# A four-layer graph network on one core: masks made four blocks ahead, left-over weights made in the first sweep and carried through DRAM, row sums in another PSUM bank, two kept pairs loaded early

## What is computed

```python
# layer 0
Ax = adj @ h;  x = x + 1 - 0.1 * h - 0.01 * sum(h * Ax, axis=1)
# layer 1: two hops
g = h
for k in range(2):
    g = tanh(concatenate([adj @ g, g], axis=1) @ W[k])
x = x + g
# layer 2: weights from the rank of a neighbour within its row
mask = (adj != 0);  rank = cumsum(mask, axis=1);  deg = rank[:, -1:]
k = minimum(deg, 100);  pos = rank - (deg - k)
w = mask * where(pos > 0, 0.5 ** (k - pos), 0)
x = x + w @ (h @ weight) + bias
# layer 3
u = tanh(concatenate([h, t]) @ W1 + b1) @ W2 + b2
XB = h @ B.T
x = x + u + adj @ XB - sum(adj, axis=1) * XB
```

## Time and profile before

| | |
|---|---|
| median of three runs | 791.98 us |
| the profiled execution, its own time | 788.66 us |
| its span | 786.6 us |
| PE, DVE, ACT, POOL busy | 91%, 60%, 23%, 21% |
| DMA | 280.96 MB, 357 GB/s mean |
| chain that ended last | PE 51%, DMA 31%, DVE 8%, POOL 4% |

### The profile page before, as it was taken

One profiled execution on the slowest core, in us unless ns is written; L12 is line 12 of the kernel. 1 busy time (PEld: TensorE's weight loads), 2 busy tenths in 40 slices (PEclk: granted clock), 3 DMA queues, 4 the chain that ended last, 5 costly groups with the idle time before them and its releaser, 6 DMA issues.

```text
span 786.6 us, 10295 instructions
## 1 busy us (share of the span) xinstructions
PE 714.9 (91%) x3752; PEld 287.1 (36%) x3752; DVE 468.5 (60%) x789; ACT 182.8 (23%) x279; POOL 168.7 (21%) x172
## 2 busy tenths in 40 slices
PE   1999999999899999999999967888888889999997
PEld 0333333333334333344444432333333333433333
DVE  5677666767988878555566625878888831111111
ACT  2000000000001000001010015777777731111111
POOL 5011110012000000012112232343454414222231
PEclk9999999999999999999999987999999999999999
DMA  9799999999999999999999948888999979999994
GB/s 372 312 423 420 421 419 420 421 418 366 345 387 408 385 383 374 379 358 359 362 370 367 350 192 330 328 309 316 341 349 339 330 247 373 351 369 369 367 367 191
DMA packets 48659, 280.96 MB, mean 357 GB/s; under 512 B 5985, under 2 KB 15329, under 8 KB 15713
## 3 DMA queue, kind: packets, MB, share of 16 engines
q1 hardware_dynamic: 38754, 271.39, 88.6%
q10 hardware_dynamic: 9856, 8.92, 3.5%
HBM read 275.56 MB, written 4.73 MB: 356 GB/s over the span
## 4 chain that ended last, share of the span: by engine, by line
PE 51%; DMA 31%; DVE 8%; POOL 4%; issue 4%; ACT 1%; SPq 0%; ACTq 0%; DVEq 0%; POOLq 0%
PE accA L993 34%; DMA land<-adj_blocks 15%; DMA cache<-adj_blocks 8%; DMA uS<-counts 5%; PE spare L1025 4%; DMA xin<-x_rows 3%; PE accA L1036 3%; DVE uS L835 2%; PE nat L926 2%; PE tr L902 2%; POOL rstd L495 2%; PE spare L1008 1%; PE nat L922 1%; DVE uS L825 1%; PE nat L918 1%
## 5 line engine op out<-in xcount | busy, mean ns | idle before, releaser
L993 PE MATMUL accA<-land,X 128*64 128x512 f32 x1536 | 370.1, 600 | 10.7 <-DMA land<-adj_blocks 7.8
L825 DVE TENSOR_TENSOR uS<-uS,land 128x512 f32<-128x512 f32 x192 | 133.1, 693 | 65.4 <-DMA land<-adj_blocks 56.1
L993 PEld LDWEIGHTS accA<-land,X 128*64 128x64 f32 x1536 | 103.0, 137 | 187.6 <-issue 136.2
L835 DVE TENSOR_SCALAR uS<-land 128x1024 bf16<-128x1024 f32 (+1 forms) x192 | 134.2, 747 | 53.6 <-DMA land<-adj_blocks 52.6
L993 PE MATMUL accA<-cache,X 128*64 128x512 f32 x512 | 126.5, 602 | 15.2 <-DVE X L867 12.5
L502 POOL TENSOR_TENSOR hS<-tS 128x256 f32<-128x256 f32 x32 | 25.6, 802 | 475.5 <-DVE tS L706 475.5
L407 ACT ACTIVATE wS<-spare 128x1024 uint16<-128x1024 f32 x112 | 108.6, 1033 | 56.2 <-PE spare L1025 56.0
L1025 PE MATMUL spare<-uS,triA 128*128 128x512 bf16 x256 | 78.5, 389 | 30.7 <-DMA uS<-counts 11.0
L1036 PE MATMUL accA<-wS,X 128*128 128x512 bf16 x256 | 77.7, 386 | 0.0
L583 ACT ACTIVATE rowsT<-tr 128x256 f32<-128x256 f32 x40 | 15.4, 385 | 236.2 <-PE tr L902 236.2
L993 PEld LDWEIGHTS accA<-cache,X 128*64 128x64 f32 x512 | 36.6, 138 | 83.2 <-issue 76.9
(11 more groups left out here) (78 smaller groups left out, 465.8 us busy)
## 6 DMA issues: line engine op xcount, KB each, us to landing
land<-adj_blocks SPq DMA_DIRECT2D x240, 1024.0 KB, 7.6
cache<-adj_blocks SPq DMA_DIRECT2D x16, 1024.0 KB, 12.3
xin<-x_rows ACTq DMA_DIRECT2D x32, 128.0 KB, 5.5
x_rows<-zS ACTq DMA_DIRECT2D x24, 128.0 KB, 5.0
cache<-x_rows SPq DMA_DIRECT2D x1, 1024.0 KB, 4.9
loadjS<-adj_blocks SPq DMA_DIRECT2D x64, 8.0 KB
uS<-counts SPq DMA_DIRECT2D x64, 4.0 KB
out_rows<-zS ACTq DMA_DIRECT2D x8, 128.0 KB, 7.3
```

The costliest lines, as they stand in the source:

```text
L825: nc.vector.tensor_tensor(total, total, of[:, i * W:(i + 1) * W], ALU.add)\
L835: nc.vector.tensor_scalar(masks(b)[0:rows, :], block_of(p, c, b)[0:rows, :], 0.0, None, ALU.not_equal)\
L993: last = nc.tensor.matmul(accA[k * D:(k + 1) * D, c % 2, :], tile(X[p % 2], TQ * b + k), of[:, k * W:(k + 1) * W], start=(b == 0), stop=(b ...
```

## The change

What it does, part by part:

1. `LEAD = 4`: in L2 DVE makes masks 0 to 3 ahead of block 0, and at block b the mask of block b + 4. Its two evictions per column (`EVAC_LAG` 3 to 1) stand one block behind their own instead of three.
2. The left-over weights are made in L0. SP loads the left-over rows of adj for a column in one DMA (`left_adjacency`, from a new input that the host lays out), DVE combines them with the counts in one operation more, ACT makes the weights and writes them to DRAM. In L2 SP fetches them per column in one DMA; GpSimd's `left_over` is gone. The matmul has 64 rows instead of 32.
3. The 127th rows go to `loS` in 32 small DMAs, four per column (`left_rows_of`): for columns 0 to 5 ahead of the loads of L1B's columns 2 to 7, for 6 and 7 in L2.
4. `sums_p` moves to the bank of `nat`; its matmuls come ahead of the row matmuls of the same stage, and the first triangle no longer waits for `rowsum`.
5. The kept pairs of column 1 are loaded in L0 ahead of pair 6 of column 0.

The diff, cut to its core:

```diff
+L0_LOADS = [(c, k) for c in range(NC) for k in range(PAIRS)]
+for _k in cached_pairs(1):
+    L0_LOADS.remove((1, _k))
+    L0_LOADS.insert(L0_LOADS.index((0, 6)), (1, _k))
...
+LEAD = 4
...
-EVAC_LAG = 3
+EVAC_LAG = 1
...
-        sums_p = spare[:, 0, 0:4]
+        sums_p = nat[:, CH:CH + 4]
...
         @block.sync
+            def left_adjacency(c):
+                if c:
+                    sp.wait_ge(left_later, c)
+                else:
+                    sp.wait_ge(cleared, 1)
+                sp.dma_start(loadjS[1:2 * NT:2, :], left_in_d[:, c * W:(c + 1) * W]).then_inc(left_adj, 16)
+
             def left_over(c):
-                if c:
-                    sp.wait_ge(left_ready, c)
-                rows = adj_in.rearrange("(b p) (t w) -> p b t w", p=P, t=2 * TQ)
-                for k in range(PAIRS):
-                    sp.dma_start(loadjS[4 * k:4 * k + 4, :], rows[LAST, c * PAIRS + k]).then_inc(left_in, 16)
-                sp.dma_start(locntS[:, :], tile_counts[c, :, 1]).then_inc(left_in, 16)
+                if c >= 2:
+                    sp.wait_ge(weighed, c - 1)
+                sp.dma_start(left_weights(c), left_d[c]).then_inc(left_in[c % 2], 16)
+
+            def left_rows_of(c):
+                sp.wait_ge(cleared, 1)
+                sp.wait_ge(copy_used, copied_no(L1B, c, 1) + 1)
+                for t in range(4 * c, 4 * c + 4):
+                    sp.dma_start(loS[2 * t + 1:2 * t + 2, :], tile16(t)[LAST:P, :]).then_inc(left_rows, 16)
...
             def step(p, c, before, before2):
                 if p == L2 and c == 0:
                     sp.wait_ge(counts_out, 16 * NC)
+                    sp.wait_ge(left_out, 16 * NC)
                     left_over(0)
+                    left_over(1)
                     after_masks(0)
-                for k in range(PAIRS):
+                if p == L1B and c >= 2:
+                    left_rows_of(c - 2)
+                if (p, c) == (L1A, 0):
+                    left_adjacency(NC - 1)
+                for c, k in [(c, k) for k in range(PAIRS)] if p != L0 else L0_LOADS[c * PAIRS:(c + 1) * PAIRS]:
...
                     sp.dma_start(land[:, n % LAND, :], rows).then_inc(landed[n % LAND], 16)
+                    if p == L0 and k == 5 and c:
+                        left_adjacency(c - 1)
...
         @block.scalar
+                    act.wait_ge(left_later, c + 1)
+                    if c:
+                        act.wait_ge(left_out, 16 * c)
+                    nc.scalar.activation(loweightS, lolaterS, ACT.Relu, bias=wt("full", rows=(0, D)),
+                                         scale=-BIT * BIT).then_inc(left_made, 1)
+                    act.wait_ge(left_made, c + 1)
+                    act.dma_start(left_d[c], loweightS).then_inc(left_out, 16)
...
         @block.vector
+                        dve.wait_ge(left_adj, 16 * (c + 1))
+                        dve.wait_ge(count_ready, c + 1)
+                        if c:
+                            dve.wait_ge(left_made, c)
+                        nc.vector.scalar_tensor_tensor(out=lolaterS, in0=loadjS, scalar=0.0, in1=countS,
+                                                       op0=ALU.is_equal, op1=ALU.max).then_inc(left_later, 1)
...
+                if p == L0:
+                    mask(p, c, b)
+                if p == L2 and NQ * c + b + LEAD < NQ * NC:
+                    mask(p, (NQ * c + b + LEAD) // NQ, (b + LEAD) % NQ)
...
+                if p == L2 and c == 0:
+                    for b in range(LEAD):
+                        mask(p, c, b)
...
         @block.tensor
+                    if p == L1B:
+                        pe.wait_ge(totalled, totalled_no(L1B, c, TOTALS[L1B][-1]))
+                        if c:
+                            pe.wait_ge(rowsum_ready, c)
+                        for j in range(4):
+                            last = nc.tensor.matmul(sums_p[:, j:j + 1], totals(c)[:, j * P:(j + 1) * P], wt("ones"),
+                                                    start=True, stop=True)
+                        last.then_inc(sums_done, 1)
...
-                if p == L2 and c == 0:
-                    pe.wait_ge(rowsum_ready, NC)
```

More of the change, by code:

```diff
@@ L221, in sweep_steps, with gnn_kernel @@
     finish((L3, NC - 1))
-def gnn_kernel(nc, x_in, adj_in, wts_in, tri_in, out):
+def gnn_kernel(nc, x_in, adj_in, left_in_d, wts_in, tri_in, out):
     x1_d = nc.dram_tensor("x1_rows", (P, NT * D), F32, kind="Internal").ap()
@@ L251, in gnn_kernel @@
         later = sb("later", [P, 4 * NT], BF16)
-        loS = sb("loS", [NT, P], F16)
-        loadjS = sb("loadjS", [NT, W], F32)
-        locntS = sb("locntS", [NT, W], BF16)
-        lowS = sb("lowS", [NT, 2 * W], U16)
+        loS = sb("loS", [2 * NT, P], F16)
+        lowS = sb("lowS", [2 * NT, 2 * W], U16)
         accS = sb("accS", [P, W], F32)
@@ L276, in gnn_kernel @@
         countS = wS[0:D, :].bitcast(BF16)[:, 2 * W:3 * W]
+        loadjS = wS[0:D, :].bitcast(F32)[:, 2 * W:3 * W]
+        lolaterS = wS[0:D, :].bitcast(BF16)[:, 3 * W:4 * W]
+        loweightS = wS[0:D, :].bitcast(U16)[:, 6 * W:7 * W]
         hidS = uS[:, :].bitcast(F32)[:, 0:2 * W]
@@ L325, in gnn_kernel @@
         counts_in = [sem(f"counts_in{i}") for i in range(MASKS // 2)]
-        left_in, left_rows, left_step, left_ready = sem("left_in"), sem("left_rows"), sem("left_step"), sem("left_ready")
+        left_adj, left_later, left_made, left_out = sem("left_adj"), sem("left_later"), sem("left_made"), sem("left_out")
+        left_in = [sem(f"left_in{i}") for i in range(2)]
+        left_rows, cleared = sem("left_rows"), sem("cleared")
         tri_done = sem("tri_done")
@@ L445, in after_masks @@
                     counts_to[0] = i + 1
-                if g % PAIRS == 3 and g // PAIRS + 1 < NC:
+                if g % PAIRS == 3 and 1 < g // PAIRS + 1 < NC:
                     left_over(g // PAIRS + 1)
-                if g == 6:
-                    sp.wait_ge(copy_used, copied_no(L1B, NC - 1, 1) + 1)
-                    sp.dma_start(left_d, X[1][LAST:P, :].bitcast(F16)).then_inc(left_rows, 16)
-                    sp.wait_ge(left_rows, 16)
-                    sp.dma_start(loS[:, :], left_d.rearrange("o (t w) -> (o t) w", w=2 * D)).then_inc(left_rows, 16)
+                if g in (2, 6):
+                    left_rows_of(NC - 2 if g == 2 else NC - 1)
             counts_to = [0]
@@ L552, in step @@
                         split_rows(before[1])
-                if p == L2 and c + 1 < NC:
-                    left_over(c + 1)
                 if p == L3 and c:
@@ L567, in _ @@
                 inverse_root(g, 8, pro_stat(3, g), pro_stat(2, g))
+            nc.gpsimd.memset(loS[:, :], 0.0)
+            nc.gpsimd.memset(loadjS, 0.0).then_inc(cleared, 1)
             sweep_steps(step, lambda before: None)
@@ L928, in epilogue @@
                     last.then_inc(nat_done, 1)
-                    if p == L1B:
-                        pe.wait_ge(totalled, totalled_no(L1B, c, TOTALS[L1B][-1]))
-                        if c:
-                            pe.wait_ge(rowsum_ready, c)
-                        for j in range(4):
-                            last = nc.tensor.matmul(sums_p[:, j:j + 1], totals(c)[:, j * P:(j + 1) * P], wt("ones"),
-                                                    start=True, stop=True)
-                        last.then_inc(sums_done, 1)
                 if at == ("transpose" if p == L3 else HT_PE.get(p, None)):
@@ L1052, in step @@
                     count(NC - 1, NQ - 1)
-                if p == L1B and c == 0:
+                if p == L2 and c == 0:
                     pe.wait_ge(count_ready, NC)
-                if p == L2 and c == 0:
-                    pe.wait_ge(rowsum_ready, NC)
                 if s >= 2:
@@ L1088 @@
     blocks = blocks.reshape(NC * PAIRS * P, PAIR)
+    left = np.ascontiguousarray(host(adj)[:, LAST::P].T)
     wts = np.zeros((P, NCOLS), np.float32)
@@ L1122 @@
     put("ones", np.ones((P, 1), np.float32))
+    put("full", np.full((P, 1), NEIGH * BIT, np.float32))
     i, j = np.arange(P)[:, None], np.arange(P)[None, :]
@@ L1128 @@
     tri[:, P:P + 2 * NT:2] = 1.0
-    tri[:, P + 1:P + 2 * NT:2] = BIT
+    tri[:, P + 1:P + 2 * NT:2] = 1.0 / BIT
     tri[LAST, P + 2 * NT] = 1.0
     nc = bacc.Bacc("TRN2", target_bir_lowering=False, num_devices=1, dynamic_dma_scratch_size=SCRATCH)
-    arrays = {"x_rows": x_rows, "adj_blocks": blocks, "weights": wts, "triangles": tri}
+    arrays = {"x_rows": x_rows, "adj_blocks": blocks, "adj_left": left, "weights": wts, "triangles": tri}
     args = [nc.dram_tensor(n, a.shape, mybir.dt.from_np(a.dtype), kind="ExternalInput").ap()
```

48 lines of the change are left out of this document (18 added, 30 removed).

## The result

The changed kernel takes **868.29 us** (median of 4 runs, 864.16 to 873.41); the kernel before took 793.51 in the same comparison (788.62 to 800.94). The ratio is 1.097 (95% interval 1.088 to 1.106): slower, as forecast, but 75 us slower where the forecast was 40, and outside its range. The profiled executions are 868.56 and 788.66 us, with spans of 866.8 and 786.6.

A forecast was written before the change was run, and what follows sets the result against it. It took L0 as bound by DMA, L1B by PE, and L2 by nobody in particular, its chain of waits passing through the counts transfer. Terms summed to +41 us on 788.66, 829.7, adjusted toward the median to 832; range 812 to 850.

The forecast's parts named there:

- the counts loop: L2: small counts transfer, asked for only after the triangle four pairs earlier, limits a column to 16.8 us.
- step 5: L2's last seven columns: masks ahead, fewer DMA issues and no GpSimd left-over steps give 17.5 us a column, -19.3 us.
- Step 1: L1B, columns 2 to 7: SP's wait for split rows holds back loads, PE stalls and restarts slowly, +60.9 us.
- The clock term: L1B: after each stall PE restarts at half speed, 2.0 us lost a column, in six columns.
- Step 2: L0 to L1A: the wait in left_adjacency(7) ahead of L1A's first load delays its loads, +4.7 us.
- Step 3: L0: two kept pairs loaded early fill idle DMA, gaining 4.1 us, against 2.7 of left-over weight transfers; -1.4 us.
- Step 4: First column of L2: earlier sums and loads, triangles not waiting for rowsum, masks before the epilogue; -3.9 us.
- the wait costs nothing: Rival, L1B: the split is already done when SP gets there, so the kernel is faster, 772 us; chance 0.07.
- SP's place delays no load: Rival, L1B: SP reached the loads late anyway, so its wait does not delay them; no chance of its own given.
- The clock is lost once: Rival, L1B: same stall, but the clock loss is paid once, not six times; 822 us, chance 0.15.
- L2 gives little: Rival, L2: counts land behind more loads, columns take 19 us; 842 us, or 847 with slower loS DMAs; chance 0.15.

The follow-up runs named there:

- the first experiment: The changed kernel with the four small DMAs and their wait moved behind the loads of each L1B column; 788.83 us, ratio to before 0.994.
- a4_before_with_the_wait: The kernel before plus SyncE's wait for the split rows ahead of the loads of L1B's columns 2 to 7, no transfer; 851.01 us, ratio 1.074.

## Why the prediction was right and wrong

**What bounds the kernel** was read rightly for L0 and L1B. For L2 the forecast listed PE, the counts loop and DMA as bounds and left out DVE; see step 5. (Its floor of 16.6 us for a column also lies under its own 16.8 for the counts loop.)

**Step 1, L1B, +60.9: right in mechanism, place and number of columns; mis-sized, +84.6.** The end of the split (4.24 us into the column, forecast 4.2), SP's stop and the landing were as worked out. Two terms were too small. The stall is 9.55 a column, not 8.45: the four DMAs take 0.60 us each and not the 0.35 of `loadjS`, which is 1.0 of the 1.1. The clock term was 2.0 and PE's busy time shows 4.6: in four of the six columns the clock took 11 to 13 us to come back, where the earlier trace rows shows 4. The sum, 14.1, is what the columns lost. The forecast took the kindest row at hand for both terms, and both are paid six times: 6 x 3.65 = 21.9, and 1.8 that it took off for stalls of before, which the columns counted here (17.81 us each) don't have. That is 23.7 of the 39 us between the change of span (80.2) and the forecast's sum (41).

The rule cited from the Trainium skill (page "TensorE: Matmul & The Clock Gate", section "HAM oscillation"), that a DMA wait in every tile throttles the engine anew each time, holds here: the granted clock falls in all six columns. That the loss is half of the throttled time holds for PE's busy time (half of 11 to 13 us is near the 5 to 6.5 of a long column), but not for the kernel's: with the clock kept up only 1.9 us a column came back.

**Step 2, L1A, +4.7: right**, +5.4, and 5.0 of it came back by moving one call behind three loads.

**Step 3, L0, -1.4: wrong in sign, +3.8.** The gain from the early pairs (4.1) was counted as DMA time saved, though the text itself said that PE's pace gates the next loads; 0.8 to 2.9 came of it. The small transfers were costed by their bytes, 0.16 us each and 2.7 in the sweep; one more of them cost 0.4 to 0.6 us.

**Step 4, first column of L2, -3.9: right in sign**, -2.3. PE waits 5.4 us at 571.88 for `hS`, the rows of L1B's last column, which the walk through the engines did not follow.

**Step 5, seven columns, -19.3: about half**, -10.2. The masks are short again and the waits for them are gone, as forecast (a mask takes 684 ns from the cache). The column stops at 18.5, because DVE's ten microseconds between the eviction of block 4 and `hS` lie in one order. The step that failed is the list of bounds: it had PE at 16.4 (17.0 measured), no bound for DVE's own sequence, and the counts loop as the nearest, of which PE's waits for counts in the seven columns are 0.9 us.

**The rivals.** None was the case as it stood. That the wait costs nothing and that SP's place delays no load fell with the first experiment. "The clock is lost once" fell: it is lost six times. "L2 gives little" had the size of L2 nearly right (18.8 a column, against its 19) and the price of the small DMAs, though it gave another reason. The range left out the case that several terms are too small at once, although each had been read from a favourable row.

## What to carry to other kernels

Before a wait is put into the program of an engine that issues loads, ask what stands behind it: the loads of this column had been 8.8 us early, and moving the same wait behind them turned 868 into 789 us. A transfer of 64 KB or of one row is not costed by its bytes in a sweep that DMA bounds, nor its issue by the cheapest issue seen. And an engine that is 79% busy, as DVE is in the columns of 18.50 us, can still be the bound by its order: the test is to move one consumer, and see whether the wait goes or takes another name.

## What the runs showed of the hardware

- The clock's return after one and the same idle of 9.5 to 9.6 us took 3 to 4 us in two columns and 11 to 13 in four others of the same kernel; after idles of 6.75 to 7.36 us it took 3 to 5 in all six of a4_before_with_the_wait.
- Four DMAs of a row of 256 B each, from one partition of SBUF to others, took SP 2.40 us to issue, against 2.84 for eight of `loadjS` from DRAM.
- A second read of 32 rows of 2 KB added 0.6 us to a DMA-bound column (one profile), a second write of 64 KB in 64 rows 0.4 (one profile), where their bytes are 0.16 at 420 GB/s.
